# Projections of an attention block: first rows of Wk and of the context ahead of x, batch 0's V ahead of its turned x

## The reference

```python
x = x + tanh(g_xattn[0]) * xattn(layernorm(x), ctx, Wq, bq, Wk, bk, Wv, bv, Wo, bo)
x = x + tanh(g_ffn[0]) * ffn(layernorm(x), gate_weight, w1, b1, w2, b2)
# xattn, 16 heads of 16:
q, k, v = query @ Wq + bq, key_value @ Wk + bk, key_value @ Wv + bv
out = softmax(q @ k.T / 4) @ v @ Wo + bo
# ffn: 8 experts of hidden width 1024, y = gelu(x @ w1.T + b1) @ w2.T + b2,
# summed with gates = logits * (logits >= the 6144th smallest)
```

## Time and profile before

| | us |
|---|---|
| median of 3 runs | 1924.23 (1922.54 to 1926.05) |
| the profiled execution | 1925.5 |
| its span, first to last instruction | 1923.7 |
| TensorE busy in the span | 1870.8 (97%) |
| VectorE busy | 1294.5 (67%) |
| ScalarE busy | 1280.5 (67%) |
| GpSimd busy | 146.4 (8%) |

### The profile page before, as it was taken

One profiled execution on the slowest core, in us unless ns is written; L12 is line 12 of the kernel. 1 busy time (PEld: TensorE's weight loads), 2 busy tenths in 40 slices (PEclk: granted clock), 3 DMA queues, 4 the chain that ended last, 5 costly groups with the idle time before them and its releaser, 6 DMA issues.

```text
span 1923.7 us, 25738 instructions
## 1 busy us (share of the span) xinstructions
PE 1870.8 (97%) x8868; PEld 1342.3 (70%) x8868; DVE 1294.5 (67%) x2279; ACT 1280.5 (67%) x2145; POOL 146.4 (8%) x327
## 2 busy tenths in 40 slices
PE   7999999999999999999999999999999999999998
PEld 6733333343367887888788788888878888887886
DVE  6788888888757666556665655665565576556555
ACT  4447777777765556766676766767677676767665
POOL 6201011101124500000000000000000000000000
PEclk9979999999999999999999999999999999999999
DMA  8932332222212353233322323333232433322321
GB/s 288 365 79 81 83 86 73 80 80 73 70 45 89 150 206 118 88 120 142 127 107 96 110 88 132 142 116 115 88 110 88 146 132 115 112 88 88 112 107 57
DMA packets 97245, 220.84 MB, mean 115 GB/s; under 512 B 31314, under 2 KB 49492, under 8 KB 87892
## 3 DMA queue, kind: packets, MB, share of 16 engines
q1 hardware_dynamic: 97108, 219.12, 33.0%
HBM read 178.57 MB, written 40.24 MB: 114 GB/s over the span
## 4 chain that ended last, share of the span: by engine, by line
PE 83%; DVE 7%; ACT 3%; issue 2%; POOL 0%; DVEq 0%; ACTq 0%; POOLq 0%
PE ps_y L2167 32%; PE ps_h L2114 28%; PE ps_t L834 5%; PE ps_h L2087 5%; PE ps_y L2099 4%; PE ps_o L845 4%; DVE low L981 3%; PE ps_m L870 1%; ACT probs_T L1158 1%; PE ps_s L823 1%; DVE attn L1004 1%; PE ps_m L856 1%; DVE x_res L1014 1%; DVE x_lo L1065 1%; DVE xn_b L1057 1%
## 5 line engine op out<-in xcount | busy, mean ns | idle before, releaser
L2467 DVE TENSOR_TENSOR h_lo<-gelu,h_hi 128x512 fp32r<-128x512 f32 x512 | 353.0, 694 | 437.0 <-ACT h_hi L2367 405.7
L2114 PE MATMUL ps_h<-x_hi,w_pair 128*128 128x512 f32 x1568 | 562.7, 393 | 1.8 <-ACT gelu L2364 1.0
L2364 ACT ACTIVATE gelu<-early,b 128x512 f32<-128x512 f32 x336 | 243.3, 724 | 229.6 <-DVE early L2616 221.0
L2114 PEld LDWEIGHTS ps_h<-x_hi,w_pair 128*128 128x128 f32 x1568 | 294.4, 188 | 78.1 <-issue 6.1
L981 DVE TENSOR_REDUCE low<-ps_s 128x1 f32<-128x512 f32 x512 | 321.4, 682 | 31.9 <-PE ps_s L823 29.5
L2367 ACT ACTIVATE h_hi<-gelu 128x512 fp32r<-128x512 f32 x448 | 283.5, 633 | 41.9 <-ACT gelu L2364 1.1
L2114 PE MATMUL ps_h<-x_lo,w_pair 128*128 128x512 f32 x784 | 309.4, 395 | 0.0
L1158 ACT ACTIVATE probs_T<-ps_t 128x512 f32<-128x512 f32 x384 | 207.8, 600 | 94.0 <-PE ps_t L834 92.2
L2616 DVE TENSOR_TENSOR early<-ps_h,copy 128x512 f32<-128x512 f32 x336 | 230.6, 686 | 49.3 <-PE ps_h L2114 49.3
L823 PE MATMUL ps_s<-k_st,q_st 48*128 48x512 f32 x512 | 205.6, 479 | 3.1 <-SPq L727 2.0
L2167 PE MATMUL ps_y<-h_hi,w_lo 128*128 128x512 f32 x512 | 202.7, 396 | 0.0
(11 more groups left out here) (263 smaller groups left out, 2532.4 us busy)
## 6 DMA issues: line engine op xcount, KB each, us to landing
x_hi<-blocks_scratch SPq DMA_DIRECT2D x28, 1024.0 KB, 5.1
x_lo<-blocks_scratch SPq DMA_DIRECT2D x28, 1024.0 KB, 8.8
x_hi<-blocks_scratch SPq DMA_DIRECT2D x28, 768.0 KB, 6.7
x_lo<-blocks_scratch SPq DMA_DIRECT2D x28, 768.0 KB, 10.2
gate<-gates_scratch SPq DMA_DIRECT2D x64, 256.0 KB, 3.2
q_st<-q_scratch SPq DMA_DIRECT2D x192, 64.0 KB, 2.3
k_st<-k_scratch SPq DMA_DIRECT2D x192, 64.0 KB, 2.3
k_scratch<-k_hl SPq DMA_DIRECT2D x8, 1024.0 KB, 5.5
```

Of the source, the lines that this page charges most:

```text
L2114: mm = pe.matmul(bank, w[wp], x[xp], start=start and n == 0, stop=n == 2, skip_group_check=not start)
L2364: act.activation(gelu[:, c % GELUS, :], src, ACT.Gelu_apprx_tanh, bias=b1[p][:, j:j + 1]).then_inc(gelu_done, 1)
L2467: dve.tensor_tensor(h_lo[:, j % RING, :], gelu[:, j % GELUS, :], h_hi[:, j % RING, :].bitcast(F32), ALU.subtract).then_inc(h_ready, 1)
```

## The change

SyncE issues the top 128 rows of Wk and of batch 0's context first, then x, then, once two fills are done, the rest of Wk with its bias and the rest of the context; Wv comes ahead of Wq. The top of the context has semaphores of its own, and its high and low parts are made apart from the rest. K of batch 0 runs all its products of k = 0 (both output tiles) and then those of k = 1, waiting for the rest of the context in between. V of batch 0 stands ahead of its turned x on TensorE and ScalarE. VectorE splits the context's top and Wk ahead of the statistics of batch 0, and Wv ahead of Wq. Left out here: the three semaphores, GpSimd's first four fills in the new order (Wk, context 0, Wv, context 1), and the two numbers of `w_split` on TensorE that follow from Wv ahead of Wq.

```diff
--- before.py
+++ after.py
...
@@ -156,17 +159,23 @@
 
-            def load_with_bias(w, w_in, b_in):
+            def load_top(w, w_in):
                 sp.dma_start(w_raw[w][:, 0, :], io[w_in][0:P, :]).then_inc(w_loaded[w], 16)
+
+            def load_rest(w, w_in, b_in):
                 sp.dma_start(w_raw[w][0:rest, 1, :], io[w_in][P:CTX, :]).then_inc(w_loaded[w], 16)
                 sp.dma_start(w_raw[w][rest:rest + 1, 1, :], io[b_in].rearrange("(a n) -> a n", a=1)).then_inc(w_loaded[w], 16)
 
+            load_top("wk", "Wk")
+            sp.dma_start(ctx_t[0][:, 0, :], io["ctxT"][0:1, 0:P, :].rearrange("a c t -> (a c) t")).then_inc(first_top_loaded, 16)
             load_x(0)
+            sp.wait_ge(filled, 2)
+            load_rest("wk", "Wk", "bk")
+            sp.dma_start(ctx_t[0][0:rest, 1, :], io["ctxT"][0:1, P:CTX, :].rearrange("a c t -> (a c) t")).then_inc(ctx_loaded[0], 16)
+            load_top("wv", "Wv")
             sp.wait_ge(filled, 4)
-            load_with_bias("wk", "Wk", "bk")
-            load_ctx(0)
+            load_rest("wv", "Wv", "bv")
             sp.dma_start(w_raw["wq"][:], io["Wq"].rearrange("(k p) n -> p k n", p=P)).then_inc(w_loaded["wq"], 16)
-            load_with_bias("wv", "Wv", "bv")
             sp.dma_start(bq[:], io["bq"]).then_inc(small_loaded, 16)
...
@@ -287,11 +295,24 @@
                 b = bb * 2 + p
-                if isinstance(bb, int) and b == 0:
+                if b == 0:
                     pe.wait_ge(w_split, 1)
-                pe.wait_ge(ctx_split, b + 1)
+                    pe.wait_ge(first_top_split, 1)
+                else:
+                    pe.wait_ge(ctx_split, b + 1)
                 wait(pe, k_split, b)
                 wk, ctx_parts = (w_hi["wk"], w_lo["wk"]), (ctx_hi[p], ctx_lo[p])
+                if b == 0:
+                    parts = [(a, c) for a, c in ((0, 0), (0, 1), (1, 0))]
+                    for k in range(KT):
+                        if k == 1:
+                            pe.wait_ge(ctx_split, 1)
+                        for m in range(KT):
+                            for i, (a, c) in enumerate(parts):
+                                mm = pe.matmul(ps_k[:, m, :], wk[a][:, k, m * P:(m + 1) * P], ctx_parts[c][:, k, :],
+                                               start=(k == 0 and i == 0), stop=(k == 1 and i == len(parts) - 1))
+                    mm.then_inc(k_in_psum, 1)
+                    return
                 for m in range(KT):
...
@@ -322,9 +343,9 @@
                     if first:
+                        values(bb, p)
                         pe.wait_ge(filled, 12)
                         turn(bb, p)
-                        values(bb, p)
                     project_q(bb, p)
@@ -346,9 +367,16 @@
                     act.wait_ge(more_filled, IN_FLIGHT - 1 + b - 2)
-                act.wait_ge(ctx_loaded[s], b // IN_FLIGHT * 32 + 32)
+                act.wait_ge(ctx_loaded[s], b // IN_FLIGHT * 32 + (32 if s else 16))
                 wait(act, v_in_psum, b - 1)
+                if b == 0:
+                    act.activation(ctx_hi[p][:, 1, :], ctx_t[s][:, 1, :], ACT.Copy).then_inc(ctx_hi_done, 1)
+                    return
                 act.activation(ctx_hi[p][:], ctx_t[s][:], ACT.Copy).then_inc(ctx_hi_done, 1)
+
+            def take_first_top():
+                act.wait_ge(first_top_loaded, 16)
+                act.activation(ctx_hi[0][:, 0, :], ctx_t[0][:, 0, :], ACT.Copy).then_inc(first_top_hi_done, 1)
 
@@ -380,9 +408,9 @@
                     if first:
-                        take_x(bb, p)
                         act.wait_ge(filled, 14)
                         take_v(bb, p)
+                        take_x(bb, p)
                         act.wait_ge(bq_ready, 1)
@@ -390,10 +418,11 @@
 
+            take_first_top()
             split_weights("wk", 3, 1.0)
             take_ctx(0, 0)
+            split_weights("wv", 3, 1.0)
             split_weights("wq", 1, -(HDIM ** -0.5))
-            split_weights("wv", 3, 1.0)
             act.wait_ge(small_loaded, 48)
@@ -423,8 +452,15 @@
 
+            def split_first_top():
+                dve.wait_ge(first_top_hi_done, 1)
+                dve.tensor_tensor(ctx_lo[0][:, 0, :], ctx_t[0][:, 0, :], ctx_hi[0][:, 0, :].bitcast(F32), ALU.subtract).then_inc(first_top_split, 1)
+
             def split_ctx(bb, p):
                 dve.wait_ge(ctx_hi_done, bb * 2 + p + 1)
+                if (bb, p) == (0, 0):
+                    dve.tensor_tensor(ctx_lo[0][:, 1, :], ctx_t[0][:, 1, :], ctx_hi[0][:, 1, :].bitcast(F32), ALU.subtract).then_inc(ctx_split, 1)
+                    return
                 dve.tensor_tensor(ctx_lo[p][:], ctx_t[(bb * 2 + p) % IN_FLIGHT][:], ctx_hi[p][:].bitcast(F32), ALU.subtract).then_inc(ctx_split, 1)
@@ -464,11 +500,12 @@
 
+            split_first_top()
+            split_weights(0, "wk", 1.0)
             statistics(0, 0)
-            split_weights(0, "wk", 1.0)
             split_ctx(0, 0)
-            split_weights(1, "wq", -(HDIM ** -0.5))
-            split_weights(2, "wv", 1.0)
+            split_weights(1, "wv", 1.0)
+            split_weights(2, "wq", -(HDIM ** -0.5))
             normalise(0, 0)
```

More of the change, by code:

```diff
@@ L98, in build_project @@
         first_loaded = n.sem("a_first_loaded")
+        first_top_loaded = n.sem("a_first_top_loaded")
         w_loaded = {w: n.sem(f"a_{w}_loaded") for w in w_raw}
@@ L103, in build_project @@
         ctx_split = n.sem("a_ctx_split")
+        first_top_hi_done = n.sem("a_first_top_hi_done")
+        first_top_split = n.sem("a_first_top_split")
         xn_hi_done = n.sem("a_xn_hi_done")
@@ L200, in _ @@
         def _(pool):
-            for w in ("wk", "wv"):
+            for p, w in enumerate(("wk", "wv")):
                 pool.memset(w_raw[w][rest:P, 1, :], 0.0).then_inc(filled, 1)
-            for p in range(2):
                 pool.memset(ctx_t[p][rest:P, 1, :], 0.0).then_inc(filled, 1)
@@ L301, in project_q @@
                 if isinstance(bb, int) and b == 0:
-                    pe.wait_ge(w_split, 2)
+                    pe.wait_ge(w_split, 3)
                 pe.wait_ge(xT_ready, b + 1)
@@ L312, in values @@
                 if isinstance(bb, int) and b == 0:
-                    pe.wait_ge(w_split, 3)
+                    pe.wait_ge(w_split, 2)
                 wait(pe, v_ready, b)
```

## The result

The changed kernel takes 1927.52 us (median of 20 runs) against 1924.30 of the kernel before on the same chip: ratio 1.0016, interval 1.0009 to 1.0023, so 1.7 to 4.4 us slower. (One of the 20 took 3483 us; the ratio leaves it out.) Forecast was 1927.0 and +2.8.

The account below looks back on a forecast made before the run. Bound: the chain of statistics, root and normalisation that releases TensorE's unbroken block. Later statistics +3.2 and a shorter root -0.4 gave +2.8 us, from 1924.23 to 1927.0 us; range 1922.5 to 1929.8.

Parts of the forecast that it names:

- The bound: Projection stage: batch 2's normalisation, ending a chain of statistics, roots and normalisations, releases TensorE's unbroken block; hardly 0.3 us slack.
- the signs to look for: Projection stage: statistics at about 7.7, root's end 14.5, normalisations 14.6, 23.1 and 32.4, block's head 33.9.
- Step (2), Wk's landing: Batch 0's statistics on VectorE wait for Wk's split; Wk lands at 6.3, so they end 3.2 us later.
- Step (3), the root: Batch 0's root on GpSimd: two weight splits beside it in place of three, -0.4 us.
- Step (4): Batch 0's normalisation on VectorE still takes 2.53 us beside GpSimd's fills; batch 1's root still 4.50 us.
- What was covered: TensorE: K starts 2.2 us earlier, V ends about 15.2, Q starts about 20.9; waits for the chain hide the gain.
- rival C: Chain delayed more: Wk lands at 6.8, splits stop the root, Q may run slowly; +4.2 us, 1928.4; 22%.
- A (K decides): TensorE's own earlier work releases the block, so K's 2.2 us earlier start is kept: 1922.0; 8%.
- B: Chain delayed little: Wk lands at 5.3, splits do not touch the root; +0.9 us, 1925.1; 20%.
- D: Attention stage: the granted clock's return shifts relative to the work, 1 to 2 us either way; 5%.

Follow-up runs that it names:

- e1: The changed kernel with batch 0's statistics back ahead of the two splits on VectorE, x still third in SyncE's queue; ratio to the kernel before 1.0007.
- e3: The changed kernel with x issued first and batch 0's statistics first on VectorE, the rest of the change kept; ratio to the kernel before 0.9998.
- e5: The changed kernel with GpSimd's fills for context tiles 2 and 3 and the attention tile moved later, out of the chain; ratio 1.0009.
- e10: e9 with GpSimd's fills of context tiles 2 and 3 also moved behind batch 1's root; 1922.29 us, ratio to the kernel before 0.9990.
- e9: e7 with ScalarE's wait for the gates, scaled bias and tanh moved to just before its copy of Q; 1922.97 us, ratio to the kernel before 0.9988.
- e4: The kernel before with only V of batch 0 ahead of its turned x and Wv ahead of Wq; ratio to the kernel before 1.0003.
- e7: The kernel before with the same edits of GpSimd's fills as e5; ratio to the kernel before 0.9990.
- e6: The changed kernel with the splits of Wv and Wq moved behind batch 0's normalisation and batch 1's statistics on VectorE; one execution, 1931.34 us.
- e2: The changed kernel with x issued first again, VectorE still splitting Wk ahead of the statistics; ratio to the kernel before 1.0015.

## Why the prediction was right

- *The bound.* Right: a block of TensorE work with no gap, released by batch 2's normalisation, and the chain of statistics, root and normalisation behind it. Every link moved by the same 3.5 to 3.6 us. What touched the chain moved the head: e1, e3 and e5 by 0.9, 2.7 and 0.6 against the changed kernel, e10 by 0.7 against e9. What hardly did (e4) moved it by 0.3 against the kernel before. e7 shows the limit of this: with a shorter chain, ready at 30.28, TensorE's own late Q set the head at 31.63.
- *The size.* The head moved by 3.59, not 2.8: the signs to look for came 0.7 to 0.8 us late all along (root's end 15.29 for 14.5, normalisations 15.32, 23.86 and 33.22 for 14.6, 23.1 and 32.4, head 34.65 for 33.9). The median came at 1927.52, 3.2 above that of the kernel before. That it lies nearer to the forecast than the head does is luck: its interval, 1.7 to 4.4, holds both.
- *Step (2), Wk's landing.* Too small by 0.3. I took 6.3 between bounds of 5.3 and 6.8; ScalarE started at 6.73, so it was nearer to the byte count of the earlier trace rows than to the earlier issue. Neither is a fixed number: with the same DMAs issued at the same times it started at 6.83 in e1, 7.26 in e5 and 7.42 in e6, beyond my upper bound. Statistics ended 3.47 us later, not 3.2. x itself was no bound: in e1 it is there at 6.53.
- *Step (3), the root.* The term with the wrong sign: I took 0.4 us off for one split fewer beside it, and the root got 0.13 longer. I had priced the two weight splits and put the context's half at nothing; the trace has all three on the root's first steps, which take 0.57, 0.65 and 0.65 in place of 0.20. Their number does not give the price exactly. By the root's length less 4.5 us: one split 0.4 (e6); three 1.3, 1.6 and 1.6 (changed, e2, e5); four 1.2 to 1.6 (before, e4, e7, e9, e10); five 1.9 and 2.0 (e1, e3). The sum by the rule of the Trainium skill (SBUF — State Buffer, Who interferes with whom) was 3.6, and 3.59 is what was measured, but that is in part luck: its root would be 0.4 longer, too much by 0.27, and the landing that it was added to too small by 0.27. The rule itself the traces bear out: e2's step of 1.77 us, and one of 1.77 in e5, agree with an instruction that stands still for whole splits.
- *Step (4).* Right: 2.53 and 1.39 and 4.5 us again (17.77, 19.31 to 23.82).
- *What was covered.* Right in its result, not in its times: K began at 8.14 (7.7), V ended at 16.4 (15.2), as the slow spacing lasted 5.3 us and not 4.4; Q began at 21.56 (20.9) and ran slowly, as rival C had allowed. So TensorE did not wait for batch 1's xn, as I had said it would: it came to that turn only at 26.82. Batch 2's normalisation was later than all of it by 0.98 us.
- *Rivals.* A (K decides) fell: K 1.7 us earlier gave nothing. B needed a landing at 5.3 and a root without disturbance; neither came. C had the root's disturbance right and reached 4.2; the measured value lies between it and mine. D happened in single executions (last section). Whether it cancels over the 20 runs is not shown: a head 3.59 later and a median 1.7 to 4.4 higher leave room for anything from -1.9 to +0.8 us.

## What to carry to other kernels

Starting the busiest engine's first work earlier is worth nothing if the engine then waits for a chain of small steps on the others: find what releases the first stretch that runs without a gap, and protect the head of that chain, here the DMA and the statistics of batch 0. When an instruction is moved off such a chain on its engine, look at what is queued behind its new place: twice here the fills just held back the next root. A tiny GpSimd step that takes three times as long as its twins (0.57 to 0.65 us for 0.20 here) is a reason to look for a VectorE instruction beside it that reads two tiles of the on-chip memory, SBUF.

## What the runs showed of the hardware

The changed kernel's profiled span is only 0.7 us longer (1924.4 against 1923.7), although its attention stage begins 3.6 later. The rest goes with the granted clock of the attention stage. Mean over 84 to 160 us (the last but two column), changed kernel and e1:

```profile
84.00:160.00 76.00, 69.92 (x342) 33.28 (x340) 62.52 (x115) 37.30 (x72) 3.57 (x26) 0.84 0.45 140
```
```profile
84.00:160.00 76.00, 70.73 (x320) 32.85 (x319) 59.82 (x112) 36.10 (x70) 3.56 (x26) 0.78 0.42 134
```

By windows of 2 us the clock falls from 2.4 to 1.2 GHz 0.2 to 3.1 us after the first score and comes back between 119 and 131 us. Where it stays at half for about 24 us, the span from the first score to the end is 1828.7 us (changed), 1828.7 (e4) and 1829.2 (e7); for 27 us, 1828.6 (e3); for 31 us, 1831.6 (before), 1830.3 (e2), 1831.4 (e9) and 1830.2 (e10); for 34 us, 1831.5 (e1) and 1831.9 (e5). The attention work is the same in all of them, and the difference, 1 to 3 us in one execution, is as much as the whole effect of the change. What decides the moment was not tried.

The slow spacing of batch 0's Q is not decided by the wait ahead of it alone: Q ran slowly, for all or most of its length, after 2.50 us (changed) and 2.23 us (e7), but at full spacing after 2.57 us (e4) and 3.38 us (e3).

GpSimd's fills are not harmless beside VectorE: the same normalisation takes 2.53 us with them and 1.38 without (e5, e7, e9, e10).
